# An adaLN block on one core: quantizer slots from a table with the last norms apart, split waits in the down projection, VectorE's residual add for the last four pairs, and new order tables

## The chip, the cores and the metric

One core of one Trainium2 chip. The time is device microseconds of one execution; runs of one kernel are compared by their median.

## The reference

`x` is 4 x 1024 x 128, fp32. `c` gives six rows of 128 per batch (shifts, scales, gates). Cut to what matters:

```python
h = _layernorm(x) * (1 + ca) + sa
q, k = _l2norm(heads(h @ Wq)), _l2norm(heads(h @ Wk)); v = heads(h @ Wv)      # 16 heads of 8
beta, fast, slow = sigmoid(h @ Wb), sigmoid(h @ Wfd + bfd), sigmoid(h @ Wsd + bsd)
flux = clip(sigmoid(silu((k * beta) @ Wtf1 + btf1) @ Wtf2 + btf2), 0.01, 0.99)
M_fast, M_slow = ...   # sums over the sequence of k*beta*w (x) v*beta, w from suffix sums of log decays
o = alpha * (q @ M_fast) + (1 - alpha) * (q @ M_slow);  alpha = 0.5 + 0.3 * flux
x = x + ga * (o @ Wo)
h = _layernorm(x) * (1 + cb) + sb
gate, up = fp4(h) @ fp4(w_gate).T, fp4(h) @ fp4(w_up).T                       # 128 -> 352
x = x + gb * (fp4(silu(gate) * up) @ fp4(w_down).T)                           # 352 -> 128
```

`fp4` quantizes and dequantizes blocks of 16 columns: the scale is the block's largest magnitude over 6, values go to the grid 0, 0.5, 1, 1.5, 2, 3, 4, 6.

## The kernel before

The 4096 tokens are 32 tiles of 128, taken as 16 pairs (`PAIRS`), four to a batch. Every engine executes its own list of steps, written out by hand in the table `ORDER`; a step `F1:12` is the function `F1` of that engine for pair 12. Steps of different engines meet through semaphores that count, and nothing is re-ordered while it runs: a step that waits holds up all that follows it on its engine.

The steps of one pair, in the order of the data:
- `XN`, `PX`, `PP`: first norm, transpose, and the product of each tile with `wcat` (496 columns: q, k, v and gates). ScalarE copies the keys, values and gates out of PSUM and squares q and k; VectorE sums the squares (`PP` there, L826).
- `GA`, `GD`, `GS`, `GE` on ScalarE: the gates of a batch. `GA` and `GD` use exp and log, `GS`, `GE` and later `F1` use silu and tanh. `tables(name)` (L522 to L527) issues a table load, L526, where the step before used the other set.
- `V`, `GG`, `O1`, `O2`, `O3`: state, output and first residual; VectorE's `O3` (L916 to L934) adds the residual to `x_all` and takes the statistics of the second norm, GpSimd's `O3` (L454) the power, VectorE's `L1` and ScalarE's `L1` (L680) the norm, GpSimd's `L1` (L462, L466) scale and shift into `q_x`.
- The quantizer, by slots. `Q` on VectorE is the front half: block maxima (L952), scales (L957), reciprocals (L960). `QR` on GpSimd scales (L475), `QA` on ScalarE takes the magnitude (L691), `QT` on VectorE rounds with two operations (L968, L971), `QO` on GpSimd scales back (L487). A slot `s` takes columns of two sources at once: the norm of pair `s - 4` (256 columns) and the FFN's hidden values of pair `s - 6` (704 columns). Slots 4 and 5 hold a norm alone, 6 to 19 both (960 columns), 20 and 21 an FFN alone. Two halves of `q_x`, `q_r` and `q_o` are used in turn, by `s % 2`.
- `N4` on TensorE transposes the quantized norm, ScalarE copies it (L697), `F1` multiplies with gate (L1166) and up (L1168) weights; ScalarE's `F1` is silu of the gate (L706), VectorE's `F1` the product with up (L982), written to `q_x`.
- `F3` on TensorE transposes the quantized hidden values (L1177), ScalarE copies them (L714), two copies for a pair. `F4` on TensorE adds `x_all` through a product with the identity (L1187) and the down projection (L1189) in one bank `Y2`; ScalarE's `F4` copies it to `x_all` (L720), and SyncE stores it (L332).

TensorE writes to three banks that ScalarE empties (`pa`, counted by `a_free`) and two that VectorE empties (`pv`, counted by `v_free`); a bank is used again when the step that had it has been read. The lines that give the slots:

```python
Q_NORM, Q_FFN = 4, 6
...
            lo = 0 if s - Q_FFN >= 0 else QF0
            return slice(lo, QCOLS if s - Q_NORM < PAIRS else QF0), ...
```

## Time and profile before

| | us |
|---|---|
| median of 3 runs | 214.57 (213.33 to 214.69) |
| the profiled execution | 214.73 |
| its span | 213.0 |
| TensorE, VectorE, GpSimd, ScalarE busy | 185.1, 174.6, 152.9, 144.6 |
| chain that ended last: TensorE, ScalarE, waiting for nothing shown, GpSimd, VectorE | 49%, 18%, 13%, 9%, 6% |

The span is the stretch that the trace covers; the execution's own time has 1.7 us more around it. Rows name engines PE (TensorE, PEld its weight loads), DVE (VectorE), ACT (ScalarE), POOL (GpSimd) and the line of the kernel. "Busy" sums the instructions of an engine; the idle time in front of an instruction carries the name of what released it.

### The profile page before, as it was taken

To read this page: it belongs to the slowest core of one execution; us is meant where nothing else is said; L and a number is where in the kernel's file an instruction comes from. 1 tells how busy PE (TensorE), PEld (TensorE's weight loads), DVE (VectorE), ACT (ScalarE), POOL (GpSimd) and SP (SyncE) were. 2 spreads that over 40 slices of the span, in tenths; PEclk is the share of its full clock that TensorE was granted. 3 is DMA by queue.
4 is the path that set the end of the run, shared out by engine and by line. 5 is a ranking of instruction groups with operands and counts; after the bars stand their busy time and mean duration, and the time that the engine had idled before them with its cause. 6 is when DMAs were issued, how large, how long until landed. Compare 5 with 4: busy or idle time off the path is not lost.

```text
span 213.0 us, 3498 instructions
## 1 busy us (share of the span) xinstructions
PE 185.1 (87%) x948; PEld 134.6 (63%) x948; DVE 174.6 (82%) x436; ACT 144.6 (68%) x326; POOL 152.9 (72%) x187
## 2 busy tenths in 40 slices
PE   2699959699999999879669999989999996989973
PEld 1544426366787748539538777868786683875863
DVE  3795998956898999999999999899998896876730
ACT  2369898998998999969753637655726456653741
POOL 6367353797688878979997975977867967666530
PEclk9999987999999999999999999999999999999999
DMA  6980000000000000000000100010001000010011
GB/s 166 247 211 5 0 2 0 5 0 0 0 5 0 0 0 2 0 0 5 25 0 0 29 0 25 2 29 0 25 11 42 0 25 25 3 51 26 3 49 49
DMA packets 11499, 5.66 MB, mean 27 GB/s; under 512 B 1684, under 2 KB 11352, under 8 KB 11480
## 3 DMA queue, kind: packets, MB, share of 16 engines
q1 hardware_dynamic: 11168, 5.31, 9.1%
q8 instruction: 8, 0.13, 0.3%
...
q14 instruction: 11, 0.09, 0.1%
...
## 4 chain that ended last, share of the span: by engine, by line
PE 49%; ACT 18%; issue 13%; POOL 9%; DVE 6%; DMA 2%; SPq 0%; POOLq 0%; DVEq 0%; ACTq 0%
PE pa L1089 10%; PE pa L1166 6%; PE pv L1168 5%; PE pa L1189 4%; PE pv L1130 4%; POOL q_o L487 3%; PE pg L1113 3%; POOL q_r L475 3%; PE pa L1177 3%; PE pa L1139 3%; DMA wmod_sb<-in_L_wmod_dram 2%; ACT L526 2%; PE pv L1149 2%; ACT xn L680 2%; PE pa L1187 2%
## 5 line engine op out<-in xcount | busy, mean ns | idle before, releaser
L475 POOL TENSOR_TENSOR q_r<-q_x,q_rs 128x960 f32<-128x960 f32 (+2 forms) x18 | 29.6, 1644 | 14.4 <-DVE q_rs L960 14.3
L1089 PE MATMUL pa<-wcat,hT 128*128 128x496 f32 x64 | 32.2, 631 | 5.4 <-ACT sq L606 3.6
L487 POOL TENSOR_TENSOR q_o<-q_r,q_sp 128x960 f32<-128x960 f32 (+2 forms) x18 | 29.5, 1642 | 7.3 <-DVE q_r L971 6.4
L1166 PE MATMUL pa<-guT,hqT 128*128 128x352 f32 x64 | 25.3, 477 | 4.8 <-ACT hqT L697 4.7
L1189 PE MATMUL pa<-wdg,fqT 128*128 128x128 f32 x192 | 26.7, 275 | 0.0
L706 ACT ACTIVATE sgl<-pa 128x352 f32<-128x352 f32 x32 | 14.5, 461 | 15.1 <-PE pa L1166 12.9
L1168 PE MATMUL pv<-guT,hqT 128*128 128x352 f32 x64 | 24.3, 462 | 0.3 <-DVE oc L913 0.3
L438 POOL TENSOR_TENSOR vs<-kvg,cw 128x256 f32<-128x256 f32 x32 | 20.0, 651 | 5.8 <-DVE cw L864 5.8
L1189 PEld LDWEIGHTS pa<-wdg,fqT 128*128 128x128 f32 x192 | 24.0, 192 | 0.0
L1089 PEld LDWEIGHTS pa<-wcat,hT 128*128 128x128 f32 x64 | 12.0, 205 | 16.8 <-ACT sq L606 7.1
L691 ACT ACTIVATE q_A<-q_r 128x960 f32<-128x960 bf16 (+2 forms) x18 | 16.0, 888 | 8.3 <-POOL q_r L475 5.3
L982 DVE TENSOR_TENSOR q_x<-sgl,pv 128x352 f32<-128x352 f32 x32 | 15.7, 511 | 5.9 <-PE pv L1168 5.0
L968 DVE SCALAR_TENSOR_TENSOR q_x<-q_A,q_r 128x960 f32<-128x960 f32 (+2 forms) x18 | 18.5, 1026 | 2.5 <-ACT q_A L691 2.4
L952 DVE TENSOR_REDUCE q_am<-q_x 128x60 f32<-128x960 f32 (+2 forms) x18 | 18.7, 1039 | 1.0 <-POOL q_x L466 0.6
L971 DVE SCALAR_TENSOR_TENSOR q_r<-q_A,q_x 128x960 f32<-128x960 f32 (+2 forms) x18 | 18.8, 1046 | 0.6
L1166 PEld LDWEIGHTS pa<-guT,hqT 128*128 128x128 f32 x64 | 11.0, 189 | 11.3 <-ACT hqT L697 7.4
L1130 PE MATMUL pv<-wm,hT 128*128 128x256 f32 x64 | 16.5, 385 | 1.9 <-DVE q_x L982 1.7
L714 ACT ACTIVATE fqT<-pa 128x384 f32<-128x384 f32 x32 | 13.9, 486 | 6.1 <-PE pa L1177 6.1
L603 ACT ACTIVATE kvg<-pa 128x368 f32<-128x368 f32 x32 | 15.2, 475 | 3.8 <-PE pa L1089 3.1
L1168 PEld LDWEIGHTS pv<-guT,hqT 128*128 128x128 f32 x64 | 12.0, 190 | 7.6 <-DVE oc L913 1.2
L680 ACT ACTIVATE xn<-x_all,nmrb,rstdb 128x128 f32<-128x128 f32 x32 | 13.9, 485 | 3.2 <-DVE nmrb L941 3.0
L462 POOL TENSOR_TENSOR q_x<-xn,mb 128x256 f32<-128x256 f32 x16 | 11.8, 739 | 5.5 <-issue 5.1
...
## 6 DMA issues: line engine op xcount, KB each, us to landing
...
```

The costliest lines, as they stand in the source:

```text
L438: g.tensor_tensor(vs[:, t].rearrange("p a (h d) -> p a h d", d=DK), vt.unsqueeze(1).to_broadcast([P, 2, H, DK]), cw[:, t].unsqueeze(3).to_ ...
L475: g.tensor_tensor(blocks(q_r[:, s % 2, c]), blocks(q_x[:, s % 2, c]), spread(q_rs[:, s % 2, n]), ALU.mult)\
L487: g.tensor_tensor(blocks(q_o[:, s % 2, c]), blocks(q_r[:, s % 2, c]), spread(q_sp[:, s % 2, n]), ALU.mult)\
L680: a.activation(xn2[:, i % 2, k, :], x_all[:, b, 2 * j + k, :], ACT.Identity, scale=rstdb[:, i % 2, k:k + 1], bias=nmrb[:, i % 2, k:k + 1]) ...
L952: v.tensor_reduce(q_am[:, r, n], blocks(q_x[:, r, c]), axis=AX.X, op=ALU.max, apply_absolute_value=True)\
L968: v.scalar_tensor_tensor(q_x[:, r, c], q_A[:, c], MAGIC_FLOOR, q_r[:, r, c], ALU.max, ALU.add)\
L971: v.scalar_tensor_tensor(q_r[:, r, c], q_A[:, c], MAGIC_FLOOR, q_x[:, r, c], ALU.max, ALU.subtract, reverse1=True).then_inc(S["q_q"], 1)
L1089: te.matmul(bank_a(("PP%d" % k, i))[:, 0:NCAT], hT[:, b, 2 * j + k, :], wcat[:, :], start=True, stop=True).then_inc(S["a_full"], 1)
L1130: last = te.matmul(t[:, k * 2 * D:(k + 1) * 2 * D], hT[:, b, 2 * j + k, :], wm[:, b % 2, :], start=True, stop=True)
L1166: te.matmul(bank_a(("G%d" % k, i))[:, 0:I], lhs, guT[:, 0, :], start=True, stop=True)\
L1168: te.matmul(bank_v(("U%d" % k, i))[:, 0:I], lhs, guT[:, 1, :], start=True, stop=True)\
L1189: last = te.matmul(t[:, k * D:(k + 1) * D], fqT[:, (2 * i + k) % 4, ch * P:(ch + 1) * P], wdg[:, b % 2, ch, :], start=False, stop=(ch == 2))
```

## The change

1. The slots come from a table `SLOTS` of pairs (norm, FFN): slots 0 and 1 hold norms 0 and 1, slots 2 to 13 norm `s` with FFN `s - 2`, slots 14 and 15 norms 14 and 15 alone, slots 16 to 19 FFNs 12 to 15 alone. All functions look up their slot there, and the waits that keep a half of a buffer from being overwritten look for the last slot of the same half that holds the same part (`before`).
2. In `F4` on TensorE the identity product waits only for `x_all`; the wait for ScalarE's copy stands behind it, one for each half.
3. For pairs 12 to 15 (`RESID_DVE`) the step is `F5`: `Y2` is a VectorE bank, TensorE issues no identity product, VectorE adds the bank to `x_all`, and SyncE and `F3`'s buffers wait for VectorE's side.
4. The four tables `ORDER` are written anew in their whole length. The steps are the same but for the two slots more and `F5`.

```diff
+RESID_DVE = 12
...
-        fills_v = {"O1": ["PO"], "O3": ["Y"], "F1": ["U0", "U1"]}
+        fills_v = {"O1": ["PO"], "O3": ["Y"], "F1": ["U0", "U1"], "F5": ["Y2"]}
...
+        SLOTS = [(i, i - 2 if i >= 2 else None) for i in range(14)] + [(14, None), (15, None)] + [(None, i) for i in range(12, 16)]
+        norm_slot = {n: s for s, (n, _) in enumerate(SLOTS) if n is not None}
+        ffn_slot = {f: s for s, (_, f) in enumerate(SLOTS) if f is not None}
...
+        def before(s, part):
+
+            return max((p for p in range(s) if p % 2 == s % 2 and SLOTS[p][part] is not None), default=None)
...
-                sp.wait_ge(S["a_free"], slot_a[("Y2", i)] + 1)
+                if i >= RESID_DVE:
+                    sp.wait_ge(S["v_free"], slot_v[("Y2", i)] + 1)
+                else:
+                    sp.wait_ge(S["a_free"], slot_a[("Y2", i)] + 1)
...
+            def F5(i):
+                b, j = divmod(i, NP_)
+                t = bank(("Y2", i))
+                xr = x_all[:, b, 2 * j:2 * j + 2, :]
+                v.tensor_tensor(xr, x_all[:, b, 2 * j:2 * j + 2, :],
+                                t[:, 0:2 * D].rearrange("p (t d) -> p t d", t=2), ALU.add).then_inc(S["v_free"], 1)
...
             def F4(i):
                 b, j = divmod(i, NP_)
                 t = bank_a(("Y2", i))
                 v_done(("Y", i))
-                a_done(("FT1", i))
-                pe.wait_ge(S["wdg"], b + 1)
                 for k in range(2):
                     te.matmul(t[:, k * D:(k + 1) * D], ident[:, :], x_all[:, b, 2 * j + k, :], start=True, stop=False)
+                    a_done(("FT%d" % k, i))
+                    if k == 0:
+                        pe.wait_ge(S["wdg"], b + 1)
...
+            def F5(i):
+                b = i // NP_
+                t = bank_v(("Y2", i))
+                for k in range(2):
+                    a_done(("FT%d" % k, i))
+                    if k == 0:
+                        pe.wait_ge(S["wdg"], b + 1)
+                    for ch in range(3):
+                        last = te.matmul(t[:, k * D:(k + 1) * D], fqT[:, (2 * i + k) % 4, ch * P:(ch + 1) * P],
+                                         wdg[:, b % 2, ch, :], start=(ch == 0), stop=(ch == 2))
+                last.then_inc(S["v_full"], 1)
```

Of a table one line, TensorE's last:

```diff
-        N4:12 F1:12 N4:13 F1:13 F3:10 F4:9 F3:11 F4:10 F4:11 N4:14 F1:14 N4:15 F1:15 F3:12 F3:13 F4:12 F4:13
-        F3:14 F4:14 F3:15 F4:15
+        F4:10 N4:13 N4:14 F1:13 F3:11 F1:14 N4:15 F4:11 F1:15 F3:12 F5:12 F3:13 F5:13 F3:14 F5:14 F3:15 F5:15
```

What stands in a row on VectorE before, from the products of pair 13 on (L982 the products, L952 to L960 a front half, L968 and L971 a rounding):

```order
L982 TENSOR_TENSOR q_x<-sgl,pv 128x352 x2
L952 TENSOR_REDUCE q_am<-q_x 128x60
L957 TENSOR_SCALAR q_sp<-q_am 128x60
L960 RECIPROCAL q_rs<-q_sp 128x60
L968 SCALAR_TENSOR_TENSOR q_x<-q_A,q_r 128x960
L971 SCALAR_TENSOR_TENSOR q_r<-q_A,q_x 128x960
L968 SCALAR_TENSOR_TENSOR q_x<-q_A,q_r 128x960
L971 SCALAR_TENSOR_TENSOR q_r<-q_A,q_x 128x960
L982 TENSOR_TENSOR q_x<-sgl,pv 128x352 x2
L952 TENSOR_REDUCE q_am<-q_x 128x44
L957 TENSOR_SCALAR q_sp<-q_am 128x44
L960 RECIPROCAL q_rs<-q_sp 128x44
```

And after the change, from the rounding of slot 13 on (L986 the products, L958 to L966 a front half, L972 and L975 a rounding):

```order
L972 SCALAR_TENSOR_TENSOR q_x<-q_A,q_r 128x960
L975 SCALAR_TENSOR_TENSOR q_r<-q_A,q_x 128x960
L958 TENSOR_REDUCE q_am<-q_x 128x16
L963 TENSOR_SCALAR q_sp<-q_am 128x16
L966 RECIPROCAL q_rs<-q_sp 128x16
L986 TENSOR_TENSOR q_x<-sgl,pv 128x352 x2
L972 SCALAR_TENSOR_TENSOR q_x<-q_A,q_r 128x256
L975 SCALAR_TENSOR_TENSOR q_r<-q_A,q_x 128x256
L958 TENSOR_REDUCE q_am<-q_x 128x16
L963 TENSOR_SCALAR q_sp<-q_am 128x16
L966 RECIPROCAL q_rs<-q_sp 128x16
L958 TENSOR_REDUCE q_am<-q_x 128x44
```

Norm 14 is now a front half and a rounding of 256 columns around the products of pair 12, where before it was part of a slot of 960 columns together with FFN 12.

TensorE's last steps before, from the transposes of pair 14 on (L1177 transposes, L1187 identity, L1189 down projection):

```order
L1177 MATMUL pa<-ident,q_o 128x128 x6
L1187 MATMUL pa<-x_all,ident 128x128
L1189 MATMUL pa<-wdg,fqT 128x128 x3
L1187 MATMUL pa<-x_all,ident 128x128
L1189 MATMUL pa<-wdg,fqT 128x128 x3
```

After, from the down projection of pair 13 on (L1188 transposes, L1213 down projection):

```order
L1188 MATMUL pa<-ident,q_o 128x128 x6
L1213 MATMUL pv<-wdg,fqT 128x128 x6
L1188 MATMUL pa<-ident,q_o 128x128 x6
L1213 MATMUL pv<-wdg,fqT 128x128 x6
L1188 MATMUL pa<-ident,q_o 128x128 x6
L1213 MATMUL pv<-wdg,fqT 128x128 x6
```

The identity products are gone there, the bank is one of VectorE's, and the transposes of a pair alternate with the down projection from pair 12 on.

ScalarE, the gates of batch 0 before, at the tanh of the flux (L660 `yt`; L603, L606 copies and squares of a projection, L526 a table load, L590 a copy of `PX`):

```order
L590 ACTIVATE hT<-pa,colmod 128x256
L658 ACTIVATE btf_h<-btf_b 128x1
L660 ACTIVATE yt<-hz,btf_h 128x128
L603 ACTIVATE kvg<-pa 128x368
L606 ACTIVATE sq<-pa 128x256
L603 ACTIVATE kvg<-pa 128x368
L606 ACTIVATE sq<-pa 128x256
L590 ACTIVATE hT<-pa,colmod 128x256
L526 ACT_TABLE_LOAD
```

After (L667 `yt`; L610 and L613 copies and squares, L533 a table load, L673 the copy of `wm`, L656 the silu of the hidden flux):

```order
L673 ACTIVATE wm<-pa 128x256
L533 ACT_TABLE_LOAD
L665 ACTIVATE btf_h<-btf_b 128x1
L667 ACTIVATE yt<-hz,btf_h 128x128
L610 ACTIVATE kvg<-pa 128x368
L613 ACTIVATE sq<-pa 128x256
L610 ACTIVATE kvg<-pa 128x368
L613 ACTIVATE sq<-pa 128x256
L656 ACTIVATE hmid<-hin,btf_b 128x128 x4
```

The tanh of batch 0 now stands behind the exp and log steps of batch 1, with a table load of its own. In the whole list ScalarE has L533 twelve times, where it had L526 ten times, besides the load at the start.

## Rows read from the trace of the kernel before

**Rows 1.** The page: busy time of each engine over the span
```profile
PE 185.1 (87%) x948; PEld 134.6 (63%) x948; DVE 174.6 (82%) x436; ACT 144.6 (68%) x326; POOL 152.9 (72%) x187
```

**Rows 2.** Busy time by stretch: start:end, length, then each engine's busy us (instructions)
```profile
20.00:80.00 60.00, 54.63 (x222) 35.66 (x222) 50.98 (x136) 55.31 (x133) 41.83 (x66) 0.97 0.00 1
80.00:172.30 92.30, 83.61 (x475) 64.69 (x473) 86.93 (x191) 58.22 (x123) 76.43 (x77) 1.00 0.04 11
172.30:204.30 32.00, 28.01 (x176) 22.00 (x176) 24.42 (x40) 18.64 (x42) 21.42 (x16) 1.00 0.09 26
```

**Rows 3.** ScalarE's timeline: start us, busy us, engine, line, operation
```profile
26.00 0.29 ACT L546 ACTIVATE wqT<-pa 128x128 f32<-128x128 f32 x1
26.30 1.28 ACT L526 ACT_TABLE_LOAD   x1
27.60 0.52 ACT L615 ACTIVATE eg<-zb 128x384 f32<-128x384 f32 x1
80.05 0.81 ACT L706 ACTIVATE sgl<-pa 128x352 f32<-128x352 f32 x2
```

**Rows 4.** Groups by line and form: busy us, mean ns of one, idle before, releaser
```profile
L971 DVE SCALAR_TENSOR_TENSOR q_r<-q_A,q_x 128x960 f32<-128x960 f32 x14 | 16.2, 1157 | 0.5
L971 DVE SCALAR_TENSOR_TENSOR q_r<-q_A,q_x 128x704 f32<-128x704 f32 x2 | 1.8, 892 | 0.1
L971 DVE SCALAR_TENSOR_TENSOR q_r<-q_A,q_x 128x256 f32<-128x256 f32 x2 | 0.8, 425 | 0.1
L952 DVE TENSOR_REDUCE q_am<-q_x 128x44 f32<-128x704 f32 x2 | 1.8, 886 | 0.1
L952 DVE TENSOR_REDUCE q_am<-q_x 128x16 f32<-128x256 f32 x2 | 0.8, 414 | 0.0
L923 DVE TENSOR_TENSOR x_all<-x_all,pv 128x256 f32<-128x256 f32 x16 | 6.4, 401 | 0.0
L826 DVE TENSOR_REDUCE ss<-sq 128x64 f32<-128x512 f32 x16 | 10.7, 675 | 2.0 <-ACT sq L606 2.0
L475 POOL TENSOR_TENSOR q_r<-q_x,q_rs 128x256 f32<-128x256 f32 x2 | 1.2, 622 | 0.7 <-DVE q_rs L960 0.7
L462 POOL TENSOR_TENSOR q_x<-xn,mb 128x256 f32<-128x256 f32 x16 | 11.8, 739 | 5.5 <-issue 5.1 <-ACT xn L680 0.3
L691 ACT ACTIVATE q_A<-q_r 128x704 f32<-128x704 bf16 x2 | 1.5, 766 | 0.0
```

**Rows 5.** Waits of VectorE, 172.3 to 204.3 us; then timeline rows there
```profile
DVE q_x L982 <- PE pv L1168: 4.2, 6, 1.2
...
174.44 0.41 DVE L923 TENSOR_TENSOR x_all<-x_all,pv 128x256 f32<-128x256 f32 x1
175.70 1.16 DVE L968 SCALAR_TENSOR_TENSOR q_x<-q_A,q_r 128x960 f32<-128x960 f32 x1
...
188.87 1.82 POOL L487 TENSOR_TENSOR q_o<-q_r,q_sp 128x960 f32<-128x960 f32 x1 [0.68 <-PE pa L1189]
...
193.20 0.52 DVE L982 TENSOR_TENSOR q_x<-sgl,pv 128x352 f32<-128x352 f32 x1 [0.97 <-PE pv L1168]
194.33 0.52 DVE L982 TENSOR_TENSOR q_x<-sgl,pv 128x352 f32<-128x352 f32 x1 [0.61 <-PE pv L1168]
```

**Rows 6.** Timeline of the end, 203 us to the last copy
```profile
203.10 0.88 PE L1177 MATMUL pa<-ident,q_o 128*128 128x128 f32 x6
204.36 1.39 POOL L487 TENSOR_TENSOR q_o<-q_r,q_sp 128x704 f32<-128x704 f32 x1 [1.31 <-DVE q_r L971]
206.67 0.82 PE L1177 MATMUL pa<-ident,q_o 128*128 128x128 f32 x6
207.20 0.87 ACT L714 ACTIVATE fqT<-pa 128x384 f32<-128x384 f32 x2
208.32 0.46 PE L1187 MATMUL pa<-x_all,ident 128*128 128x128 f32 x2 [0.84 <-ACT fqT L714]
210.38 0.38 ACT L720 ACTIVATE x_all<-pa 128x256 f32<-128x256 f32 x1 [2.31 <-PE pa L1189]
```

133 lines of the change are left out of this document (63 added, 70 removed).

## The prediction

> **What bounds the kernel now.** I read the page's busy shares first, then the busy time by stretch, the waits of VectorE and ScalarE, and last the timeline of the final 40 us.
>
> No engine is full over the whole span: TensorE is busy for 87% and VectorE for 82% [rows 1]. The bound changes with the stage. From 20 to 80 us (projections and gates of the first three batches) ScalarE has 55.3 of 60 us busy and TensorE 54.6, while VectorE has 51.0; the two are coupled through three PSUM banks. From 80 to 172.3 us VectorE has 86.9 of 92.3 us and is the bound: 5.4 us of idle in 92. From 172.3 us, the end of the quantizer's front half for norm 13 and FFN 11, to 204.3 us, the end of its last operation, VectorE has only 24.4 of 32.0 us [rows 2]. There the chain of one pair counts: GpSimd scales, ScalarE takes the magnitude, VectorE rounds twice, GpSimd scales back, TensorE transposes, ScalarE copies, TensorE multiplies. VectorE's largest wait is for the up-projection, 4.2 us in six waits [rows 5]. After 204.3 us VectorE has nothing left and 8.7 of the span's 213.0 us follow: the last scaling back, transposes, copies, the down projection, a copy and the store [rows 6].
>
> So three prices are wanted: what the new tables do to the ScalarE-bound stage, what the split slots do from 172 to 204 us, and what the new end does behind it.
>
> **Slots and the extra instructions.** Before, 18 slots hold 14 times norm and FFN (960 columns), two norms (256) and two FFNs (704). After, 20 slots hold 12 times 960, four times 256 and four times 704. The columns are the same; a 960 that is split pays its fixed part twice. The rounding of L971 costs 892 + 425 - 1157 = 160 ns more [rows 4]. A slot has five VectorE instructions (reduction, small multiply, reciprocal, two roundings); with 0.16 us for each as the upper bound two slots cost 1.6 us, with the two roundings alone 0.6 us, the lower one. I take 0.7 for a slot, 1.4 us for both, near the upper end, since all five are of the same engine and only the small two should pay less. The four residual adds are 0.40 us each, 1.6 us, the row of the same add on a 128x256 bank [rows 4]; they stand behind everything else that VectorE does.
>
> **Stretch from 172.3 us, step by step.** The new order puts the second residual add with its statistics for pair 15 (from 174.44 to 175.70 [rows 5], 1.3 us) ahead of this point, where before it stood behind. With the pace before it unchanged, the new point X is 172.3 + 1.3 = 173.6. Times from X, with slot numbers of the new table. A front half is taken as its reduction (0.89 us for 704 columns, 0.41 for 256 [rows 4]) and 0.7 us, for 256 columns 0.5, for the two small operations, an estimate; a rounding as two of L971 [rows 4].
> GpSimd scales slot 13 until 1.95 (1.82, its row for 960 columns [rows 5]) while VectorE rounds slot 12 until 2.3 (two of 1.15); GpSimd scales it back until 4.2, then adds the norms of pairs 14 and 15, two operations of 0.74 us each for a pair, until 5.75 and 7.4 [rows 4]. ScalarE has slot 13's magnitude at 3.4, VectorE rounds it until 5.8 (it waits 0.9) and does slot 14's front half, 256 columns, until 6.75. The up-projection of pair 12 follows the scaling back: that was 188.87 + 1.82 = 190.69 to VectorE's product at 193.20, 2.5 us, and the second product ends at 194.85, 4.15 us behind [rows 5]. So its products run from 6.75 to 8.4. Slot 14 is rounded until 9.4; the front halves of 15 and 16 until 11.95; slot 15 is rounded until 12.85. Pair 13 was scaled back at 9.9, so its products end at 14.1. From here VectorE has its work ready: front half of 17 until 15.65, rounding of 16 until 17.4, products of 14 until 18.3, front half of 18 until 19.9, rounding of 17 until 21.65, products of 15 until 22.55, front half of 19 until 24.15, rounding of 18 until 25.9. The magnitude of 19 needs the rounding of 18 and 0.77 us (L691's row for 704 columns [rows 4]), so the last rounding runs from 26.75 to 28.5. The stalls come to 2.7 us against 7.6 before. VectorE's last quantizer operation ends at 173.6 + 28.5 = 202.1, 2.2 us earlier than 204.3. Why: the norms of pairs 14 and 15 are slots of 256 columns, 0.62 us on GpSimd each time in place of 1.82 [rows 4, 5], so the last two up-projections come in while VectorE has other work.
>
> **The end, behind T = 202.1.** Before, TensorE began the transposes of pair 14 at 203.10, and the down product of a pair waited for both copies. The last pair's chain: transposes from 206.67, copies from 207.20 to 208.07, product from 208.32 (0.25 behind the copies), its last copy 210.38 to 210.76, store until 213.0, 2.24 us [rows 6]. From 208.32 to 210.38 the product took 2.06 us with two identity products; at half of the 0.46 us row each (it also holds the fill of the pipeline) 0.23 us goes twice, which leaves 1.6. It may also begin after the first copy, half of the 0.87 earlier. From the transposes to the add that is 0.53 + 0.44 + 0.25 + 1.6 = 2.8, then 0.4 for VectorE's add, 3.2 in all, against 210.76 - 206.67 = 4.1.
> What is late next: VectorE has two banks for Y2. The product of pair 14 needs the bank of pair 12, whose add runs behind the last rounding, until T + 0.45. It ends at T + 0.55 + 1.6 = T + 2.15, and the last transposes, pipelined behind it, begin at T + 2.0, though GpSimd has been done since T + 1.45 (1.39 us for 704 columns [rows 6]). The end is T + 2.0 + 3.2 + 2.25 = T + 7.45 = 209.55, against T + 8.7 before. Both parts together: 213.0 - 209.55 = 3.45 us gained. No store is added; SyncE waits for VectorE in place of ScalarE four times. Bounds of this sum: 1.2 us (the end alone, none of VectorE's 2.2) and 5.0 us (the end, plus half of VectorE's 7.6 us of stalls).
>
> **The early identity product** for the other twelve pairs: it gives TensorE up to the wait of a copy. VectorE, not TensorE, bounds that stage, so I take 0, with 0 to -1 us.
>
> **The re-written front.** ScalarE's order now holds 12 table loads in place of 10. Each row shows 1283 ns [rows 3], so 2.57 us is added to an engine that is busy for 55.3 of 60 us. What ScalarE, TensorE and VectorE do before the first gate product is the same set of steps in both tables, so nothing else shrinks. Against it: 4.7 us of ScalarE's idle time in that stage, and the gates of batch 0, now begun right behind its fourth pair instead of behind the eight modulation steps. Bounds: both loads seen in full, +2.6; idle time filled, -2.0 (a bit under half of the 4.7). I take +1.0, the larger share of one load exposed, since the first extra load stands in the fullest part and the second where ScalarE has gaps.
> The next activation follows a load at once: the load from 26.30 ends at 27.58 and the next row begins at 27.60 [rows 3]. By the Trainium skill ("ScalarE: Activation LUTs", section What ACT_TABLE_LOAD costs) a switch also pays a drain of about 1.38 us, 2.66 us in all; the load's own 1283 ns agree with this trace, the drain doesn't show in it. By that rule the two loads would be 5.3 us instead of 2.6, and this would be a rival, the third one below.
>
> The middle, 80 to 172 us, has the same VectorE work in another order and 5.4 us idle to win or lose; I take 0, with 2 us either way.
>
> **Sum.** -3.45 + 1.0 = -2.45 us against the profiled execution's 214.73, of which 213.0 is span. The median shown is 214.57, 0.16 lower; I apply the difference to the median: 212.1 us.
>
> **Rivals.**
> 1. The early gates hide both loads and the end is as worked out: 214.57 - 3.45 = 211.1, down to 209 if the middle closes gaps too. For it: ScalarE's idle time in that stage is larger than the two loads. Against: the loads stand in the chain of the gates themselves.
> 2. Slower: ScalarE's gate blocks now wait. The six gate activations of batch 0 stand right behind the copies of its last projection, and need VectorE's sum of it, 0.68 us [rows 4], and a smaller operation behind. While ScalarE waits in order, TensorE is stopped by its three banks. Some 1.2 us for both with the hand-overs (an estimate), in two of four batches, is 2.4; with both loads exposed 5.0 us, less 3.45: +1.5, 216.1 us. It decides once the first gate product's activation, at 80.05 us before [rows 3], comes more than 3.5 us later. Against: VectorE has 9 us of slack in that stage [rows 2].
> 3. The drain is real but hidden in these rows: -2.45 + 2.8 = 214.9 us. The row that follows a load leaves it no room [rows 3].
> 4. The split slots don't do what they are there for: the stalls move from the products to GpSimd, which now has 20 slots in one queue, and only the end's 1.25 us remain: -1.25 + 1.0, 214.3 us. For it: my working lets ScalarE and TensorE answer at once.
>
> **How the numbers follow.** Forecast 0.42, rival 1 0.22, rival 2 0.18, rival 3 0.02, rival 4 0.16. A measurement tells about 1%, 2.1 us, from no change. The forecast at 212.1 lies just beyond that, with its own range of 211 to 213.4: I count 0.26 of its 0.42 as faster and 0.16 as same. Faster by over 1%: 0.26 + 0.22 = 0.48. Within 1%: 0.16 + 0.16 = 0.32. Slower: 0.18 + 0.02 = 0.20; rival 3's time itself lies within 1%, but its front would hardly stay at that. The range leaves out 2 in 10: 208.8 to 216.0.
>
> **What would show it right or wrong.** In the changed profile: 12 loads beside the initial one, each 1.28 us; the first gate product's activation near 81 us (rival 1: 80 or earlier; rival 2: after 83.5); the last quantizer operation on VectorE near 203 us including the front's delay, with under 4 us of stalls in the 28.5 before it; from there to the end 7.5 us instead of 8.7. If the last stretch is as long as before, the step-by-step working is wrong; if the first gate product is early or late, the front is; if both agree and the time doesn't, the middle was re-ordered to a cost that I took as nothing.

## The result, and the profile after

The changed kernel took 218.12 us (median of 4 runs, 218.01 to 218.35), the kernel before 214.31 us beside it: a ratio of 1.019 (95% interval 1.014 to 1.025), about 4 us slower. The forecast was 212.1 us with a range of 208.8 to 216.0: wrong in sign, and outside the range. The medians and ratios of this document leave out executions over 1.5% above the fastest of the same kernel.

The page's busy shares, TensorE's granted clock in 40 slices of 5.4 us, and the shares of the chain:

```profile
PE 185.3 (86%) x932; PEld 134.2 (62%) x932; DVE 184.2 (85%) x450; ACT 144.8 (67%) x326; POOL 154.5 (71%) x191
...
PEclk9999999699999999759999999999999999999999
...
PE 34%; DVE 19%; ACT 17%; POOL 14%; issue 12%; DMA 2%; SPq 0%; POOLq 0%; DVEq 0%; ACTq 0%
```

VectorE has 14 rows more than in [rows 1] and 9.6 us more busy time, where the working gave it 3.0. TensorE's clock has two dips, and TensorE has fallen from 49% of the chain to 34%.

The same by stretch, with the last two cut at the marks of the prediction (X, and the end of VectorE's last rounding):

```profile
20.00:80.00 60.00, 52.31 (x214) 33.81 (x212) 51.74 (x129) 55.40 (x131) 39.24 (x58) 0.97 0.00 1
80.00:180.57 100.57, 89.06 (x486) 68.32 (x486) 92.71 (x200) 58.47 (x126) 81.01 (x86) 0.97 0.04 10
180.57:209.05 28.48, 25.85 (x164) 20.56 (x164) 24.78 (x45) 17.63 (x41) 20.87 (x19) 1.00 0.08 24
209.05:216.30 7.25, 3.84 (x30) 3.44 (x30) 1.50 (x4) 1.14 (x3) 1.39 (x1) 0.96 0.26 75
```

Against [rows 2] the end is what was worked out: 28.48 us from X to the last rounding (28.5 forecast), 3.7 us of it idle, and 7.25 us behind it (7.45 forecast). But X stands at 180.57 us, where 173.6 was worked out, or 174.6 with the sum's 1.0 us for the front. All of the loss, 7 us, is ahead of X.

VectorE's timeline around batch 0's flux product, and GpSimd's in the same stretch (start us, busy us, engine, line, operation, idle before):

```profile
37.83 4.43 DVE L879 TENSOR_SCALAR hz<-hmid,wtf_b 128x128 f32<-128x128 f32 x1 [1.74 <-ACT hmid L656]
42.30 1.41 DVE L882 SCALAR_TENSOR_TENSOR hz<-hmid,wtf_b,hz 128x128 f32<-128x128 f32 x3
...
36.80 4.74 POOL L449 TENSOR_TENSOR vs<-kvg,cw 128x256 f32<-128x256 f32 x8
41.50 0.63 POOL L437 TENSOR_TENSOR mrt<-mask,rt 128x256 f32<-128x256 f32 x1
...
41.27 0.52 ACT L622 ACTIVATE eg<-zb 128x384 f32<-128x384 f32 x1
44.66 0.42 ACT L625 ACTIVATE rn<-ss 128x256 f32<-128x256 f32 x1 [2.86 <-DVE ss L840]
...
46.99 1.20 POOL L421 TENSOR_TENSOR hin<-kvg,kb 128x512 f32<-128x512 f32 x1 [4.86 <-DVE kb L863]
```

The operation at 37.83 is a product of 128x128 with one scalar; before it took 0.61 us. It is issued 1.03 us into a run of nine GpSimd operations that stand back to back, and ends at 42.26, as the last of them ends (42.13). Behind it ScalarE's gates of batch 1 wait 2.86 us and GpSimd 4.86 us.

TensorE's timeline around pair 1's up-projection, and ScalarE's there:

```profile
85.64 1.03 PE L1124 MATMUL pg<-vs,kvg 128*128 128x256 f32 x4
90.84 1.54 PE L1177 MATMUL pa<-guT,hqT 128*128 128x352 f32 x2 [4.17 <-ACT hqT L702]
92.18 1.38 PE L1179 MATMUL pv<-guT,hqT 128*128 128x352 f32 x2
...
98.83 0.76 PE L1177 MATMUL pa<-guT,hqT 128*128 128x352 f32 x2
99.42 0.76 PE L1179 MATMUL pv<-guT,hqT 128*128 128x352 f32 x2
...
83.71 1.28 ACT L533 ACT_TABLE_LOAD   x1
89.52 0.97 ACT L696 ACTIVATE q_A<-q_r 128x960 f32<-128x960 bf16 x1
90.42 0.37 ACT L702 ACTIVATE hqT<-pa 128x256 f32<-128x256 f32 x1
```

TensorE waits 4.17 us for the copy at 90.42 (L702, step `N4:1`), which the new table puts behind batch 3's gate block (`GA:3`: a load and six activations) and a magnitude. After the wait two products take 1.38 us where they take 0.76 at 98.83; the granted clock of the stretch from 90 to 97 us is 0.55, so most of it ran at 1.2 GHz (the granted clock is given as a share of 2.4 GHz).

### The profile page after: what moved, and what is told of

Same layout as the page of the kernel before. It is cut to its first block, busy times and chain, and to the rows that moved or that the text cites. A ratio compares the mean times of both kernels' runs of the same rounds, so it can differ in the third digit from the quotient of the medians.

```text
span 216.3 us, 3488 instructions
## 1 busy us (share of the span) xinstructions
PE 185.3 (86%) x932; PEld 134.2 (62%) x932; DVE 184.2 (85%) x450; ACT 144.8 (67%) x326; POOL 154.5 (71%) x191
## 4 chain that ended last, share of the span: by engine, by line
PE 34%; DVE 19%; ACT 17%; POOL 14%; issue 12%; DMA 2%; SPq 0%; POOLq 0%; DVEq 0%; ACTq 0%
PE pa L1100 7%; PE pa L1177 6%; PE pv L1179 4%; POOL q_r L484 4%; ACT L533 3%; DVE q_r L975 3%; PE pv L1141 3%; DVE q_x L972 3%; DVE q_am L958 3%; POOL q_o L494 3%; ACT kvg L610 2%; DVE hz L879 2%; DMA wmod_sb<-in_L_wmod_dram 2%; POOL q_x L473 2%; DVE q_x L986 2%
## 5 line engine op out<-in xcount | busy, mean ns | idle before, releaser
L1100 PE MATMUL pa<-wcat,hT 128*128 128x496 f32 x64 | 30.4, 603 | 1.1 <-ACT sq L613 1.1
L1177 PE MATMUL pa<-guT,hqT 128*128 128x352 f32 x64 | 26.3, 494 | 5.0 <-ACT hqT L702 4.9
L1179 PE MATMUL pv<-guT,hqT 128*128 128x352 f32 x64 | 25.7, 485 | 1.1 <-DVE x_all L931 0.7
L413 POOL TENSOR_SCALAR xn<-x_all,nmean,rstd 128x128 f32<-128x128 f32 x24 | 13.5, 574 | 10.7 <-PE pa L1090 10.4
L972 DVE SCALAR_TENSOR_TENSOR q_x<-q_A,q_r 128x960 f32<-128x960 f32 (+2 forms) x20 | 18.7, 933 | 2.7 <-ACT q_A L696 2.6
L449 POOL TENSOR_TENSOR vs<-kvg,cw 128x256 f32<-128x256 f32 x32 | 19.5, 636 | 1.5 <-DVE cw L872 1.5
L1201 PE MATMUL pa<-wdg,fqT 128*128 128x128 f32 x144 | 20.0, 275 | 0.0
L986 DVE TENSOR_TENSOR q_x<-sgl,pv 128x352 f32<-128x352 f32 x32 | 15.7, 514 | 5.0 <-PE pv L1179 4.8
L975 DVE SCALAR_TENSOR_TENSOR q_r<-q_A,q_x 128x960 f32<-128x960 f32 (+2 forms) x20 | 19.2, 958 | 0.7
L958 DVE TENSOR_REDUCE q_am<-q_x 128x60 f32<-128x960 f32 (+2 forms) x20 | 18.9, 947 | 0.4
L1179 PEld LDWEIGHTS pv<-guT,hqT 128*128 128x128 f32 x64 | 12.5, 199 | 9.4 <-DVE oc L921 1.4
L1201 PEld LDWEIGHTS pa<-wdg,fqT 128*128 128x128 f32 x144 | 18.0, 192 | 0.0
L1177 PEld LDWEIGHTS pa<-guT,hqT 128*128 128x128 f32 x64 | 11.5, 198 | 10.3 <-ACT hqT L702 6.1
L1124 PE MATMUL pg<-vs,kvg 128*128 128x256 f32 x64 | 16.9, 399 | 0.0
L610 ACT ACTIVATE kvg<-pa 128x368 f32<-128x368 f32 x32 | 15.2, 476 | 1.4 <-PE pa L1100 0.7
```

The costliest lines, as they stand in the source:

```text
L610: a.activation(kvg[:, n % (KRING * T), :], t[:, D:NCAT], ACT.Copy).then_inc(S["kvg"], 1)
L958: v.tensor_reduce(q_am[:, r, n], blocks(q_x[:, r, c]), axis=AX.X, op=ALU.max, apply_absolute_value=True)\
L972: v.scalar_tensor_tensor(q_x[:, r, c], q_A[:, c], MAGIC_FLOOR, q_r[:, r, c], ALU.max, ALU.add)\
L975: v.scalar_tensor_tensor(q_r[:, r, c], q_A[:, c], MAGIC_FLOOR, q_x[:, r, c], ALU.max, ALU.subtract, reverse1=True).then_inc(S["q_q"], 1)
L986: v.tensor_tensor(q_x[:, r, k * I:(k + 1) * I], sgl[:, n % 2, :], t[:, 0:I], ALU.mult)\
L1100: te.matmul(bank_a(("PP%d" % k, i))[:, 0:NCAT], hT[:, b, 2 * j + k, :], wcat[:, :], start=True, stop=True).then_inc(S["a_full"], 1)
```

## The experiments

Three marks are used in all of them, as each stretch between two marks holds the same work in kernels of one order: **S**, ScalarE's first `wexp` activation (batch 0; at 32.00 us in the changed kernel, 32.30 in x4, 33.00 in x16, 33.23 to 33.28 in x5, x14 and x15, so that it takes out what differs between executions ahead of it; in x2 it is 34.68, behind a stretch with a granted clock of 0.6); **M1**, the start of VectorE's front half of pair 2's norm and FFN 0; **M2**, that of norm 13 and FFN 11. "Busy" is VectorE's from M1 to M2, for the same instructions (`O3:15`, 1.3 us, is among them except before). The ratio is to the kernel before beside it, whose median was 213.5 to 214.5 us in the five groups of runs. M1 and what follows are read from one profiled execution of each kernel, and that of before starts late: its S is at 35.46 us, where x1, x7, x17 and x18, with the same order up to there, have 33.31 to 33.62. Its granted clock is 0.60 from 30 to 34 us, theirs 1.00. From S to M1 it has 47.0 us as they have.

| kernel | ratio (95%) | median | M1 | M1 to M2 | busy |
|---|---|---|---|---|---|
| before | 1 | 214.3 | 82.45 | 87.93 | 82.66 |
| after | 1.019 (1.014, 1.025) | 218.12 | 85.65 | 93.06 | 85.38 |
| x1 old front and middle, new end | 0.981 (0.975, 0.988) | 210.07 | 80.66 | 88.71 | 83.25 |
| x2 new front, old middle | 1.025 (1.016, 1.033) | 219.50 | | | |
| x3 old front, new middle | 0.986 (0.977, 0.995) | 210.25 | 81.67 | 92.06 | 85.30 |
| x10 x1 with new late front | 0.997 (0.992, 1.001) | 212.99 | 83.49 | | |
| x7 early identity product alone | 0.990 (0.984, 0.995) | 212.13 | 80.55 | | |
| x8 x7 and VectorE's adds | 0.993 (0.989, 0.998) | 212.08 | 80.16 | | |
| x12 x1 without VectorE's adds | 0.978 (0.974, 0.983) | 209.47 | 80.95 | 88.66 | 83.22 |
| x11 x1 and two table loads | 0.995 (0.990, 1.000) | 213.13 | 82.87 | | |
| x16 after, two loads fewer | 1.020 (1.015, 1.026) | 217.82 | 86.68 | 92.20 | |
| x4 after, GpSimd waits for `hz` | 1.012 (1.006, 1.019) | 216.70 | 84.73 | 92.35 | |
| x5 after, copy ahead of gates | 1.011 (1.004, 1.018) | 216.56 | 86.90 | 90.59 | 85.39 |
| x9 after, wait filled (13) | 1.022 (1.019, 1.026) | 219.01 | | | |
| x13 after, two waits filled (13, 5) | 1.023 (1.019, 1.027) | 219.03 | | | |
| x14 after, wait filled (6) | 1.017 (1.010, 1.024) | 216.13 | 83.94 | 90.65 | 85.29 |
| x15 after, two waits filled (6, 2) | 1.012 (1.004, 1.019) | 216.70 | 86.94 | 90.64 | |
| x17 x12 with new middle, copy ahead | 0.997 (0.993, 1.001) | 212.43 | 80.42 | 92.59 | 87.47 |
| x18 x17 with three pauses | 0.988 (0.983, 0.993) | 210.91 | 80.32 | 91.12 | 83.96 |
| x19 x12 with one pause | 0.976 (0.971, 0.981) | 209.07 | | | |

### Which part of the tables: x1, x2, x3, x10

The four tables have places where what lies ahead is the same set of steps in both. There they can be cut and joined. x1 keeps the old order up to the up-projection of pair 10, x3 up to that of pair 0; x2 has the new front up to there, and x10 only its later half, from 50 to 80 us. For ScalarE in x1:

```diff
-        CT:0 CM:0 WK:0 PX:0 PX:1 KW:0 PX:2 PX:3 PP:0 PP:1 PP:2 PX:4 PP:3 GA:0 MB:0 PX:5 PP:4 PX:6 PP:5 PX:7 W1:0
+        CT:0 WK:0 CM:0 PX:0 PX:1 KW:0 PX:2 PX:3 PP:0 PP:1 PP:2 PX:4 PP:3 PX:5 MB:0 PX:6 PP:4 PX:7 WQ:0 GA:0
...
```

> The changed kernel's code, with the tables of before up to about 165 us (norm slot 11, all steps of which are the same in both) and the new tables from there. Theory 1 (the new end is worth what was worked out, the new front and middle lose it): 214.3 - 3.45 = 210.9 us, between 210 and 212. Theory 2 (the split slots or VectorE's residual adds cost by themselves what the change lost): 214 us or more.

> New tables up to the first gate product (about 80 us), the order of before from there to about 165 us, the new end. In the changed kernel the front half of the slot of norm 2 came 3.2 us late and that of norm 13 8.3 us. Theory 1a (front and middle lose each by their own order): 210.9 + 3.2 = 214.1 us. Theory 1b (the front makes all the loss, the middle only carries it): 210.9 + 7.0 = 217.9 us.

> The order of before up to the first gate product, the new tables from there to the end. Theory 1a: the middle's own loss, 7.0 - 3.2 = 3.8 us, over the new end alone: 214.7 us, with TensorE's pause of about 4 us near 87 us and a stretch at 1.2 GHz behind it as in the changed kernel. Theory 1b: 210.9 us and no such pause.

> The faster mixture (old front and middle, new end) with the new tables' order only for the later half of the front: from the second batch's gates (near 50 us) to the up-projection of pair 0 (near 80 us). The first half's order is the old one, with no table load more in it. Theory E (the loss is made in the first half, where VectorE's first operation of hz and the gates of batch 1 wait and the first extra load stands): 210 to 211.5 us. Theory F (half of it and more is made later, by the second load and the denser order of products): 213 us or more.

x1 is faster than both kernels, so the code, the slots and the end are a gain, 0.019 of 214 us or 4.0 us; the working had 3.45. From M1 to the end of the span x1 has 126.9 us and before 130.6, 3.6 us less. x2 is slower than the changed kernel: the front carries more than half of the loss. x3 costs 0.005 more than x1, 1 us, by the ratios, but 3.35 us from M1 to M2 in its profiled execution: that one (span 211.3) has a wait of TensorE's for the copy (3.05 us) and 1.2 GHz behind it, two others (208.4 and 208.5) had the full clock throughout. x10 costs 3.2 us more than x1 (0.997 against 0.981). Its first half has no table load more, as I had written, but its later half has both, so it tests that half's order and the loads together.

Why x2 is slower than the changed kernel, too, its trace shows. Its first gate product's activation comes 49.86 us after S, just as in the changed kernel; the next 2.4 us are lost between there and M1, in one operation (timeline of x2):

```profile
86.56 4.20 DVE L849 TENSOR_TENSOR zb<-kvg,bias 128x384 f32<-128x384 f32 x1
86.20 1.21 POOL L450 TENSOR_TENSOR vs<-kvg,cw 128x256 f32<-128x256 f32 x2
87.38 0.61 POOL L495 TENSOR_TENSOR q_o<-q_r,q_sp 128x256 f32<-128x256 f32 x1
87.96 2.38 POOL L450 TENSOR_TENSOR vs<-kvg,cw 128x256 f32<-128x256 f32 x4
```

The sum of the gates' bias took 0.82 us before and 1.85 in the changed kernel; here it takes 4.20, beside seven GpSimd operations without a gap, and ends at 90.76, 0.4 us behind them. So 2.4 of x2's time belongs to the place where its two orders meet.

### What the end gained: x7, x8, x12

x7 is the changed code with all tables and slots of before; x8 adds the four residual adds to it; x12 takes them out of x1:

```diff
-RESID_DVE = 12
+RESID_DVE = 16
...
-        ... F1:15 F3:12 F5:12 F3:13 F5:13 F3:14 F5:14 F3:15 F5:15
+        ... F1:15 F3:12 F3:13 F4:12 F4:13 F3:14 F4:14 F3:15 F4:15
```

> The changed kernel's code with all four tables and the slots of the kernel before: only the early identity product is left of the change, and only for the order in which the products of one pair are issued. Prediction's step (it gives TensorE up to the wait of a copy, VectorE bounds): 214.5 us, 0 to 1 us below. Rival (the early product closes TensorE's gaps in the last 30 us and is a good part of what the new end gained): 213 us or less, and the end behind VectorE's last rounding shorter than 8.7 us by over 0.5.

> As the run before it in this group (old tables, old slots, early identity product), and the last four pairs' residual is added by VectorE from its own banks, behind everything else that it does. Theory of the prediction (the step 'the end' gains 1.25 us by itself, the split slots another 2.2): about 213.2 us, and from VectorE's last rounding to the end of the span 7.5 us instead of 8.7. Rival (the end gains only together with the split slots, since TensorE reaches the last transposes no earlier): 214.3 us, with 8.5 us or more behind the last rounding.

> The faster mixture (old front and middle, new end with split slots) with the residual of the last four pairs back in TensorE's product and the copy back on ScalarE. By the prediction's sum the end behind VectorE's last rounding is 1.25 us longer: 211.3 us against 210.1. Rival (by the run with the adds alone, which gained nothing: the adds only move the work): 210.1 us, within 0.4.

Both times the adds gain nothing: x8 against x7 and x1 against x12 (0.978 without them, 0.981 with them). From VectorE's last rounding to the end of the span x7 has 7.2 us, x8 7.3, x12 7.2, x1 7.2, and before had 8.7. The last pair of x7, TensorE and ScalarE, timeline:

```profile
205.14 0.82 PE L1189 MATMUL pa<-ident,q_o 128*128 128x128 f32 x6
...
205.66 0.87 ACT L723 ACTIVATE fqT<-pa 128x384 f32<-128x384 f32 x2
...
205.79 0.47 PE L1197 MATMUL pa<-x_all,ident 128*128 128x128 f32 x2
...
206.21 0.94 PE L1202 MATMUL pa<-wdg,fqT 128*128 128x128 f32 x6
...
207.20 0.83 PE L1202 MATMUL pa<-wdg,fqT 128*128 128x128 f32 x6
...
208.07 0.38 ACT L729 ACTIVATE x_all<-pa 128x256 f32<-128x256 f32 x1 [1.54 <-PE pa L1202]
```

From the transposes to the end of the copy that is 3.3 us against 4.1 in [rows 6]: the first identity product (205.79) runs beside ScalarE's copies (205.66), and the down product begins behind the first of the two (206.21). The other 0.8 us is ahead of the transposes, which before stood behind the longer product of the pair in front. So x7's 2.2 us (1.1 to 3.4 by its interval) holds these 1.5. Its other 0.7 us no row gives to the edit: from M1 to the end of the span x7's trace is only 0.4 us shorter than before's, since TensorE's clock falls from 175 to 180 us in it (0.66, and 1.00 in before), and VectorE's stretch from M2 to its last rounding is 1.6 us longer by that, with two waits for the up-projection of 2.12 and 1.39 us for 1.22 and 0.61. For the same reason x1 against x7 (0.990 to 0.981, 1.8 us) isn't the price of the split slots. That is better read against before: from M2 to the last rounding before has 33.90 us, 1.3 of them `O3:15`, the changed kernel 30.34 and x1 31.00. So the slots are worth 2.3 and 1.6 us (2.2 forecast).

### The two table loads: x11, x16

x11 loads the present tables once more ahead of `GE:0` and `GE:1` in x1. x16 takes the changed kernel's two loads away; the tanh of batches 0 and 1 is left out for it:

```diff
             def GE(b):
-                tables(SILU_TABLES)
+                if b >= 2:
+                    tables(SILU_TABLES)
...
-                a.activation(yt[:, :, :], hz[:, :, :], ACT.Tanh, scale=0.5, bias=btf2_h[:, 0:1]).then_inc(S["yt"], 1)
+                    a.activation(yt[:, :, :], hz[:, :, :], ACT.Copy, scale=0.5).then_inc(S["yt"], 1)
```

> The faster mixture (old front and middle, new end: 210.1 us) with two table loads more on ScalarE, one right ahead of each of the tanh activations of batch 0 and 1, with the tables that are loaded anyway. Nothing else changes. Theory L (the two more loads are what the new front costs, the queue behind them included): at least 2.6 us, 212.7 us or more. Theory M (they fall mostly into ScalarE's idle time, and the front's loss of some 6.5 us comes from waits between VectorE, GpSimd and TensorE that the new order makes): 210.1 to 211.5 us. The prediction's step of +1.0 for both would be 211.1.

> The changed kernel without its two more table loads: the tanh of batch 0 and 1 is left out (a scaled copy of the same operands stands in its place), so that those two activations need no tables of their own. Theory L (the loads are worth in the changed kernel what they cost in the old front, 2.9 us): 214.7 to 216 us. Rival (here other waits stand behind them: VectorE's held operation and the later pause take the time back): 217 us or more.

In the old front the two loads cost all of their 2.6 us (ratio 0.981 to 0.995, 2.9 us; M1 2.2 later though x11 started earlier). In the changed kernel they cost nothing: x16's S is 1.00 us later than the changed kernel's and so is its M1, 1.03. The loads that are gone are those at 63.61 and 71.15 us of the changed kernel (that at 48.70 is at 51.59 in x16, ahead of the next silu, which needs the same tables). ScalarE in x16 behind them, timeline:

```profile
68.10 0.88 ACT L692 ACTIVATE xn<-x_all,nmrb,rstdb 128x128 f32<-128x128 f32 x2 [0.29 <-DVE nmrb L954]
...
73.10 0.38 ACT L646 ACTIVATE wexp<-pg 128x256 f32<-128x256 f32 x1 [1.14 <-PE pg L1116]
...
82.59 0.40 ACT L670 ACTIVATE yt<-hz,btf_h 128x128 f32<-128x128 f32 x1 [1.61 <-DVE hz L887]
```

What the loads give back ScalarE spends in waits for TensorE and VectorE that it doesn't have there in the changed kernel, or has shorter (1.22 us at the last row). That last row is 1.04 us later than its twin at 81.55, as S was; VectorE itself waits for 0.6 us in all between 64 and 83 us. A price found by adding a cost to one order isn't what its removal gives in another.

### The held operation: x4, and x14's profiled execution

x4 lets GpSimd start its second pair of `vs` operations only after the first `hz` product:

```diff
+                if b == 0 and n == 1:
+                    pool.wait_ge(S["hz"], 1)
                 if n == 0:
                     pool.wait_ge(S["cw"], b + 1)
```

> The changed kernel, with one wait more: GpSimd's step V1 of batch 0 waits until VectorE has done the first operation of the flux (L879), which in the changed kernel took 4.43 us while GpSimd executed eight operations back to back, against 0.61 us before. Theory 3 (VectorE was kept out by GpSimd's run and ScalarE's wait of 2.9 us in the gates of batch 1 follows from it): the operation takes under 0.7 us, ScalarE's wait goes, 218.1 - 2.5 = 215.6 us. Rival: the operation is long for another reason or ScalarE's wait costs nothing: 217.5 to 218.3 us.

VectorE and GpSimd of x4, timeline:

```profile
38.13 0.34 DVE L882 TENSOR_SCALAR hz<-hmid,wtf_b 128x128 f32<-128x128 f32 x1 [1.74 <-ACT hmid L659]
38.50 2.11 DVE L885 SCALAR_TENSOR_TENSOR hz<-hmid,wtf_b,hz 128x128 f32<-128x128 f32 x3
...
38.55 3.76 POOL L452 TENSOR_TENSOR vs<-kvg,cw 128x256 f32<-128x256 f32 x6 [0.22 <-DVE hz L882]
```

The product takes 0.34 us, ScalarE's wait is gone, and the kernel is 1.5 us faster by the ratios (its four executions took 216.35 to 216.82 us, the changed kernel's 218.01 to 218.35); from S, M1 comes 1.2 us earlier. Not all of the 2.5 expected came: the operations behind it are held in part instead, the next three products take 2.11 us for 1.41. A cleaner reading came unplanned. x14 and x15 (below) have the same order up to 85 us save two products of TensorE, and their first `hmid` activation starts at 37.25 and 37.31 us. In the profiled execution of x14 the product at 39.04 got through in 0.64 us, 1.29 us into GpSimd's run; in that of x15 it started at 39.12 and took 4.43. TensorE's clock is 1.00 in both from 36 to 44 us. The first gate product's activation is at 80.15 in one, at 83.14 in the other: the hold is worth 3.0 us, and whether it happens hangs on a moment. x14's four executions had spans from 212.1 (this one) to 216.7 us.

### The wait and the clock: x5, x9, x13, x14, x15

x5 moves the copy (with the load, `TL`) ahead of the gates, so TensorE has no such wait. x14 leaves the wait and gives TensorE products that nobody reads; x9 has 13 of them, x15 and x13 have also 2 and 5 in an earlier wait of 2.4 us. (x13, as x9 with the 5 more, was to take 213.3 to 215 us if the clock cost the time.) Two cuts, the table of x5 and `F1` of x14:

```diff
-        ... F1:0 L1:3 O2:4 GA:3 QA:2 N4:1 F1:1
+        ... F1:0 L1:3 O2:4 TL:0 N4:1 GA:3 QA:2 F1:1
...
             def F1(i):
+                if i == 1:
+                    t = bank_a(("G0", i))
+                    for _ in range(6):
+                        te.matmul(t[:, 0:I], hqT[:, 0, 0:D], guT[:, 0, :], start=True, stop=True)
                 a_done(("HQT", i))
```

> The changed kernel with one step moved on ScalarE: the copy of pair 1's transposes goes in front of the gate block of batch 3 (the table load first, as it must be somewhere), so that TensorE's up-projection of pair 1 needn't wait for those six activations. Theory A (TensorE's 4.2 us pause near 87 us and the products at 1.2 GHz behind it are paid in the time): 215 to 216 us, no pause over 2 us near there, and the granted clock of 90 to 100 us near 1.00. Theory B (VectorE bounds there, TensorE's clock costs nothing): 217.5 us or more, whatever the clock does. With A the front half of norm 13 and FFN 11 starts 2 us earlier than in the changed kernel.

> The changed kernel, and ahead of pair 1's up-projection TensorE issues 13 products of 352 columns whose result nobody reads (3.8 us by the row of two such products, 0.59 us from pair to pair) into the bank that it fills next, in the 4.2 us in which it waits there anyway. Nothing waits for less than before; only TensorE isn't idle. Theory C (the 6.6 us at 1.2 GHz behind that pause are what it costs, each product there 0.35 us instead of 0.19): granted clock 1.00 from 88 to 98 us and 215.0 to 216.3 us in place of 218.1. Theory W (the wait costs, the clock doesn't, since VectorE bounds there): 217.6 to 218.6 us.

> The earlier fill had the wrong count: a product of these operands is two rows of the trace, so that 13 took 7.7 us of a 4.2 us pause. Here 6 are issued, 3.5 us. Theory C (the products at 1.2 GHz cost the time): the four products of pair 1 begin at about 90.9 us as in the changed kernel, take 2.4 us instead of 4.9 and the time is 215.3 to 216.6 us. Theory W (VectorE and the chain bound behind that point, TensorE has room to be slow): 217.6 to 218.4 us, though the granted clock is 1.00 from 88 to 98 us.

> As the run before it in this group, and two products of 496 columns (1.8 us) in the 2.4 us wait ahead of pair 11's transposes at 36 us. Theory C: a further 1.0 to 1.9 us less, 213.5 to 215.5 us, at a mean clock of 1.00. Theory W: 217.4 to 218.4 us.

x9 and x13 told nothing by their times: a product is two rows of 0.30 us, and 13 took 7.9 us, 3.7 more than the wait. But even x9, whose real products began 3.4 us later behind M1, needed only 0.8 us more from M1 to M2 (93.88). With the right count, x14, TensorE's timeline (the second two of pair 1's four products; the first begin at 89.14, 5.2 us behind M1 as in the changed kernel):

```profile
90.43 0.76 PE L1182 MATMUL pa<-guT,hqT 128*128 128x352 f32 x2
91.02 0.75 PE L1184 MATMUL pv<-guT,hqT 128*128 128x352 f32 x2
```

The busy time by stretch of x14, with the granted clock of 1.00 behind the five engines:

```profile
90.00:100.00 10.00, 10.00 (x51) 7.29 (x49) 9.50 (x21) 5.85 (x11) 9.33 (x12) 1.00 0.01 2
```

ScalarE's copy comes as late behind M1 as in the changed kernel (4.78 and 4.77 us), the products take 0.76 us, and M1 to M2 is 90.65 us instead of 93.06: 2.4 us, and the same in x15 (90.64). All of it is gained up to the next front half; from there to M2 the two agree within 0.03 us. In x4 and x16, which leave the wait unfilled too, the clock is at half for a shorter time (back at 1.00 by 94 us in x4 and by 96 in x16, 97 in the changed kernel), and M1 to M2 is 92.35 and 92.20: there it cost 1.6 to 1.7 us. x5, whose TensorE waits 0.9 us at most there, has 90.59. So the 4.2 us wait cost nothing, and the slow products behind it cost all. (These are readings of the profiled executions, between marks; the ratios of x5 and x15, 1.011 and 1.012, go the same way, though their intervals overlap the changed kernel's; that of x14, 1.017 where its median gives 1.012, is blurred by the scatter of its start and of the hold.) The early fill gained nothing: in x15 M1 comes 53.7 us after S, as in the changed kernel, with the hold in both. The clock fell behind that earlier wait in the changed kernel (0.57 from 38 to 42 us) and not in x15 (1.00).

### The middle's order: x17, x18, x19

x17 is x12 with the new order from the up-projection of pair 0 on and the copy ahead of the gates. x18 adds three pauses, x19 adds one to x12 (`s == 4`, `nmrb` at 7):

```diff
             def QR(s):
+                if s == 2:
+                    pool.wait_ge(S["eg1"], 4)
...
             def QO(s):
+                if s == 5:
+                    pool.wait_ge(S["rt1"], 4)
+                if s == 10:
+                    pool.wait_ge(S["nmrb"], 13)
```

> Old front, the new order from the up-projection of pair 0 on with the copy of pair 1's transposes ahead of batch 3's gates, the split slots, and the last four pairs' residual in TensorE's product. If the new middle's only cost is that pause with what follows it: 209 to 210 us, not above the fastest mixture so far (209.5 us). If the order of the middle costs by itself: 211 us or more, and the front half of norm 13 and FFN 11 starts over 1 us later than in that mixture.

> As x17 (212.4 us; its VectorE is busy 4.2 us longer than the fastest mixture's for the same 188 instructions between the front halves of pair 2 and of pair 13), and GpSimd starts three of its 960-column operations only when VectorE's small operation beside them is done (0.1 to 0.5 us later each): the one beside the minimum of batch 3's gates (1.90 us for 0.30), the one beside batch 3's flux ratio (1.57 for 0.18), the one beside pair 12's statistics (1.74 for 0.10). Theory H (a small VectorE operation that is issued while GpSimd's runs is held to its end, and this is what the new middle's order costs): VectorE's busy time in that stretch falls by 4 us or more to about 83 us and the time to 208.5 to 210 us. Rival (the held time was slack, or GpSimd's later start moves it): 211.5 us or more.

> The fastest mixture (x12, 209.5 us) with one such pause: GpSimd's scaling back of slot 4 waits for VectorE's statistics product of pair 6 (1.58 us for 0.10 at 105.9 us). Theory H: that operation takes 0.1 to 0.2 us, and the time is 1.0 to 1.5 us lower, 208.0 to 208.5 us. Rival: within 0.4 us of 209.5.

Busy time by stretch, M1 to M2, of x12 and of x17. x17's TensorE had the full clock throughout, and still M1 to M2 is 3.9 us longer than x12's. VectorE's busy time for the same work says where it is:

```profile
80.95:169.61 88.66, 80.33 (x453) 61.73 (x451) 83.22 (x188) 55.13 (x116) 74.52 (x75) 1.00 0.04 11
```

```profile
80.42:173.01 92.59, 81.04 (x451) 61.90 (x451) 87.47 (x188) 54.28 (x116) 74.87 (x75) 1.00 0.04 11
```

4.25 us more for 188 instructions. x5 has the same middle behind another front: 90.59 us, 85.39 busy. The whole difference to x17, 2.0 us, is in the first slot behind M1, and from there to M2 the two agree within 0.01 us. Three of x17's instructions, each with the GpSimd row beside it (timeline of x17):

```profile
82.57 1.90 DVE L861 TENSOR_SCALAR eg<-eg 128x384 f32<-128x384 f32 x1 [0.22 <-ACT eg L624]
82.44 1.82 POOL L486 TENSOR_TENSOR q_r<-q_x,q_rs 128x960 f32<-128x960 f32 x1 [1.31 <-DVE q_rs L971]
...
116.11 1.57 DVE L895 TENSOR_SCALAR rt<-ws 128x32 f32<-128x32 f32 x1
115.83 1.82 POOL L496 TENSOR_TENSOR q_o<-q_r,q_sp 128x960 f32<-128x960 f32 x1
...
156.72 1.74 DVE L954 SCALAR_TENSOR_TENSOR nmrb<-mvb,rstdb 128x2 f32<-128x2 f32 x1
156.62 1.82 POOL L496 TENSOR_TENSOR q_o<-q_r,q_sp 128x960 f32<-128x960 f32 x1
```

Start and length added, the pairs end at 84.47 and 84.26, 117.68 and 117.65, 158.46 and 158.44. The same operations take 0.30, 0.18 and 0.10 us elsewhere. The first is what x5 hasn't (0.30 us there). The other two stand in every kernel with the new middle but x18, in the changed one too, where a kernel with the old middle has one such row (1.58 us at 105.64 in x1). Timeline of the changed kernel:

```profile
121.81 1.57 DVE L890 TENSOR_SCALAR rt<-ws 128x32 f32<-128x32 f32 x1
121.52 1.82 POOL L494 TENSOR_TENSOR q_o<-q_r,q_sp 128x960 f32<-128x960 f32 x1
...
162.41 1.74 DVE L949 SCALAR_TENSOR_TENSOR nmrb<-mvb,rstdb 128x2 f32<-128x2 f32 x1
162.32 1.82 POOL L494 TENSOR_TENSOR q_o<-q_r,q_sp 128x960 f32<-128x960 f32 x1
```

From M1 to M2 the rows that take over 0.4 us more than the shortest row of the same form add up to 5.0 us too much in the changed kernel (five rows) and to 3.0 in x1 (four). VectorE's timeline of x18:

```profile
82.45 0.36 DVE L867 TENSOR_SCALAR eg<-eg 128x384 f32<-128x384 f32 x1 [0.20 <-ACT eg L630]
...
115.51 0.18 DVE L901 TENSOR_SCALAR rt<-ws 128x32 f32<-128x32 f32 x1
115.99 1.62 DVE L960 SCALAR_TENSOR_TENSOR nmrb<-mvb,rstdb 128x2 f32<-128x2 f32 x1
...
156.09 0.15 DVE L960 SCALAR_TENSOR_TENSOR nmrb<-mvb,rstdb 128x2 f32<-128x2 f32 x1
```

VectorE is busy 3.5 us less (83.96), but M1 to M2 is only 1.5 us shorter and the ratio 0.009 lower, 1.9 us. One by one: the first pause gave 1.4 us up to the next slot's front half. The second only handed the hold on: the next small operation, at 115.99, took 1.62 us. The third gave 0.9, but 0.9 had been lost at 97 to 106 us, where TensorE's output comes later behind a stretch at 1.2 GHz (90 to 94 us) that x17 hasn't. The pause in x19 shortens its operation's stretch by 1.1 us in the trace and M1 to M2 by 0.9; its ratio is 0.976 against 0.978, which the intervals don't separate. x19 and x12 are the fastest versions, both ahead of the kernel before by over 2% in the middle of their intervals (at the near end 1.9 and 1.7%).

## Why the prediction was wrong

**"The re-written front", +1.0 us, bounds -2.0 and +2.6.** This term failed. From x1 to the changed kernel M1 moves by 5.0 us (80.66 to 85.65); against before's own trace, which has the late start, by 3.2. 3.0 of it is the one held operation (x14's against x15's execution). The two loads, which I priced, are there as said (12 of 1.28 us); they cost their 2.6 us in the old front (x11) and nothing in this one (x16). What makes the rest, 2.0 us of the 5.0, isn't told apart and stays open. My upper bound was made of the loads alone: no wait of ScalarE's for a VectorE that is itself held stood in it. That step, a front priced by ScalarE's loads and idle time alone, is what failed. Rival 2 had the right place, gates that wait for VectorE's sum, and the right sign, but batch 0 and a price from undisturbed rows; its sign, an activation after 83.5 us, didn't come either: it stands at 81.86. That sign was badly chosen, since ScalarE's delay of 1.8 us there had grown to 3.2 at M1.

**"The middle", 0 with 2 us either way.** It failed too: 4.35 us (93.06 against x1's 88.71; against before, with the 1.3 us of `O3:15` added to it, 3.8). 2.4 of it are the products at 1.2 GHz behind TensorE's 4.2 us wait (x14, x15, x5), and the rest, 1.9, goes with VectorE's busy time, 2.1 us more for the same instructions, of which the held rows make 2.0. That the held rows cost the time is shown in part: x18 takes 3.5 us of busy time away and gains 1.5. I had taken "the same VectorE work in another order" for the same time, on the rows' means. [rows 4] hide that: in the trace of before the same `nmrb` product took 1.58 us at 107.84 beside a GpSimd operation and 0.10 elsewhere. What stands beside an operation on GpSimd was part of its price, and the new table changes just that.

**Slots and "stretch from 172.3 us, step by step", 28.5 us, and "the end", 7.45.** Right: 28.48 and 7.25. Without the moved 1.3 us that is 3.67 gained against 3.45. Stalls were 3.7 us, under the 4 named, but the working had 2.7 and so 25.8 us of work, where VectorE was busy for 24.8: two misses of 1 us that cancel, so that 28.48 for 28.5 is in part luck. (By its own times the working's wait before slot 13's rounding is 1.1 us, from 2.3 to 3.4, and not 0.9.) The end's gain was put down to VectorE's adds alone; the early identity product, which I had priced at 0 "for the other twelve pairs", gives all of it without them, and the adds nothing more (x7, x8, x12). In the sum it made no difference, because either edit takes the identity products out of the last pair's chain. The adds without the early product weren't run.

**The other rivals.** Rival 1 (the front hides the loads) named a front that costs nothing; it cost 5.0. Rival 4 (split slots give nothing) falls by the stretch from M2 to the last rounding, 30.34 us against before's 32.6 without `O3:15`.

**The drain of rival 3.** By the Trainium skill ("ScalarE: Activation LUTs", section What ACT_TABLE_LOAD costs) it comes on top of a load. None of the twelve loads shows it: the one at 83.71 ends at 84.99 and a wait for VectorE follows, that at 39.98 ends at 41.26 and the next row begins at 41.27; the row ahead of it ends at 39.97.

**Sum.** 3.67 gained at the end, 5.0 and 4.35 lost ahead of it against x1: from x1's span of 207.6 to 216.3, 8.7 us (the last stretch differs by 0.6). The chance given to "slower", 0.20, was too small for a table that is re-written from top to bottom: the two unknown stretches had upper bounds of 2.6 and 2 us, and each went beyond its own.
